# A transformer layer in one kernel: the square weights of the feed-forward are loaded and split in the fill, the routing works in other tiles, and every engine's list of steps is written anew

## The reference

```python
y  = moe(x, cond)        # 8 experts (64 wide) and a shared one (128 wide), top 2 of softmax((x@wt.T + cond@wg.T) / 2)
                         # each: (leaky(x @ gate) * (x @ up)) @ down, weighted by the route
q, k, v = split(y @ W_qkv + b_qkv)
a  = (q @ k.T / sqrt(128*32)) * band(32) @ v          # no softmax
x1 = x + layer_norm(a) * ln_w + ln_b
n  = layer_norm(x1) * g_norm
Q  = l2norm(n @ Wq) * q_scale                         # 16 heads of 64
K, V = l2norm([null_k; n @ Wk]) * k_scale, [null_v; n @ Wv]    # one key and value for all heads
bias = mlp(relative position)                         # 255 positions -> 16 heads
o  = softmax(8 * Q @ K.T + bias, causal and masked) @ V
z  = layer_norm(o @ Wout) * g_out
h  = silu(z @ w1.T * s1) * (z @ w2.T * s2)
h  = gelu(h @ h1.T * t1);  h = gelu(h @ h2.T * t2)    # h1, h2: 512 x 512, the square weights
out = x1 + h @ w3.T * s3
```

## Time and profile before

| | us |
|---|---|
| median of 3 runs | 715.47 |
| lowest, highest | 715.38, 719.20 |
| the profiled execution | 719.08 |
| its span, first to last instruction | 717.1 |
| mean granted clock of TensorE | 0.983 of full |

### The profile page before, as it was taken

How to read it: one execution, slowest core, us unless ns; L and a number is a source line. 1 busy time by engine, 2 the same in 40 slices (tenths; PEclk the granted TensorE clock), 3 DMA queues, 4 the chain that set the end, 5 groups by cost and what they waited for, 6 DMA issues and landing times.

```text
span 717.1 us, 20509 instructions
## 1 busy us (share of the span) xinstructions
PE 679.9 (95%) x7232; PEld 537.5 (75%) x7232; DVE 547.5 (76%) x1719; ACT 528.1 (74%) x1629; POOL 359.6 (50%) x410
## 2 busy tenths in 40 slices
PE   5986979999999999999999999999999999899997
PEld 5855757667876778768876778777876687778897
DVE  5476999898769878698759878698759977886441
ACT  3224679579876897579876898589875989899753
POOL 3013777572549343863549344863558456932100
PEclk9898988999999999999999999999999999999999
DMA  8042400300031000400031000400040000000000
GB/s 284 9 111 90 123 2 16 82 22 1 2 87 60 1 2 12 134 3 1 3 104 43 1 3 24 122 2 1 2 118 30 1 1 25 16 17 1 17 8 8
DMA packets 33587, 28.50 MB, mean 40 GB/s; under 512 B 4288, under 2 KB 29008, under 8 KB 33104
## 3 DMA queue, kind: packets, MB, share of 16 engines
q1 hardware_dynamic: 33184, 27.19, 13.2%
q10 hardware_dynamic: 304, 0.01, 0.0%
HBM read 23.90 MB, written 3.29 MB: 38 GB/s over the span
## 4 chain that ended last, share of the span: by engine, by line
PE 57%; DVE 14%; ACT 9%; issue 7%; POOL 4%; DVEq 0%; ACTq 0%; POOLq 0%
PE ps_M L1314 30%; PE ps_z L1466 8%; DVE sb_sm L1187 5%; PE ps_S L1453 5%; PE ps_S L1438 4%; PE ps_M L1367 4%; PE ps_M L1498 3%; ACT sb_sm L830 3%; PE ps_S L1422 2%; PE ps_M L1397 2%; ACT sb_hT L795 2%; POOL sb_rq L697 1%; DVE sb_nmx L1194 1%; DVE sb_hAl L1024 1%; POOL sb_biasm L707 1%
## 5 line engine op out<-in xcount | busy, mean ns | idle before, releaser
L830 ACT ACTIVATE sb_sm<-sb_sm,sb_nmx 128x65 f32<-128x65 f32 (+3 forms) x512 | 178.1, 352 | 14.4 <-DVE sb_nmx L1194 14.1
L715 POOL TENSOR_TENSOR sb_sm<-sb_sm,sb_rden 128x128 f32<-128x128 f32 (+3 forms) x128 | 93.2, 738 | 126.4 <-DVE sb_rden L1198 126.1
L707 POOL TENSOR_TENSOR sb_biasm<-sb_bias,sb_maskn 128x128 f32<-128x128 f32 (+3 forms) x128 | 113.0, 894 | 49.6 <-DVE sb_maskn L1159 26.5
L1187 DVE SCALAR_TENSOR_TENSOR sb_sm<-ps_S,sb_rq,sb_biasm 128x65 f32<-128x65 f32 (+3 forms) x512 | 112.2, 292 | 24.0 <-PE ps_S L1438 19.5
L697 POOL TENSOR_TENSOR sb_rq<-sb_qss,sb_mhalf 128x16 f32<-128x16 f32 x32 | 93.6, 2949 | 28.8 <-DVE sb_qss L1169 28.8
L830 ACT ACTIVATION_READ_ACCUMULATOR sb_sm<-sb_sm,sb_nmx 128x1 f32 x512 | 97.1, 190 | 0.0
L1466 PE MATMUL ps_z<-sb_wout,sb_oT 128*128 128x128 f32 x512 | 69.1, 282 | 0.0
L1466 PEld LDWEIGHTS ps_z<-sb_wout,sb_oT 128*128 128x128 f32 x512 | 64.4, 193 | 4.3 <-ACT sb_oT L842 0.8
L842 ACT ACTIVATE sb_oT<-ps_S,sb_cols 128x256 f32<-128x256 f32 x128 | 52.9, 467 | 16.5 <-PE ps_S L1453 13.1
L1194 DVE TENSOR_REDUCE sb_nmx<-sb_sm 128x4 f32<-128x132 f32 (+3 forms) x128 | 59.3, 475 | 0.3
L767 ACT ACTIVATE sb_gs<-ps_M 128x512 f32<-128x512 f32 x39 | 23.2, 596 | 46.2 <-PE ps_M L1314 46.1
(11 more groups left out here) (267 smaller groups left out, 1708.6 us busy)
## 6 DMA issues: line engine op xcount, KB each, us to landing
sb_hA<-routes SPq DMA_DIRECT2D x48, 128.0 KB, 3.6
sb_vrep<-values SPq DMA_DIRECT2D x16, 256.0 KB
sb_xg<-in_xT SPq DMA_DIRECT2D x8, 256.0 KB, 3.4
sb_xs<-in_x SPq DMA_DIRECT2D x8, 256.0 KB, 6.8
sb_qs<-in_xT SPq DMA_DIRECT2D x1, 2048.0 KB, 10.5
sb_hA<-in_h SPq DMA_DIRECT2D x2, 1024.0 KB, 7.2
out_y<-sb_res SPq DMA_DIRECT2D x7, 256.0 KB, 7.0
values<-sb_vs SPq DMA_DIRECT2D x16, 64.0 KB
```

The costliest lines, as they stand in the source:

```text
L707: pool.tensor_tensor(masked_bias(j % 4)[:, :, 1:wide], relative(bias0, i), maskn[:, j // 4, 0:wide - 1].unsqueeze(1).broadcast_to([128, 4, ...
L715: pool.tensor_tensor(p, p, stat(rden, g, j).unsqueeze(2).broadcast_to([128, 4, wide - 1]), ALU.mult)\
L830: ins = act.activation(p[:, t], p[:, t], ACT.Exp, bias=least[:, t:t + 1], accum_out=total[:, t:t + 1])
L1187: ins = dve.scalar_tensor_tensor(scored(g, j)[:, t], bank(g, "sim", n, odd)[:, first:first + wide], rq[:, col:col + 1], masked_bias(j % 4) ...
```

## The change

1. The routing's scratch moves out of hA into tiles that are not yet in use: pieces of x1 and of vrep (the spread values). For that `vb` (the spread of the values) of group 0 waits until the routing is done, and the x1 of group 2 is written only after the route weights have been turned.
2. So hA is free from the start: h1 and w12 are fetched right behind the mask in the prologue of SP, and h2 after SP has waited for h1's low part; only then follow the store and the 16 loads of the turned bias. The step `hw` is gone, and `PARTS` has h1 ahead of w12: `ph.3`/`pl.3` is now h1, `.4` w12, `.5` h2, and all six are in the fill.
3. The lists of all engines and all kinds of pass are written anew. The numbers of lines behind the table are larger by one to six.

```diff
 ORDER = {
     "pe fill": """
-        lg.0 warm.0-2 pb.0-1 warm.3-6 rw.0 lg.1-2 exp.0-1 lg.3-4 exp.2 pb.2 lg.5-7 pb.3 exp.3-4 down.0 qkv.0
...
+        lg.0 pb.0 warm.0-1 pb.1 warm.2 lg.1-2 rw.0 exp.0 lg.3 exp.1 lg.4 exp.2 lg.5 exp.3 lg.6-7 warm.3 pb.2
...
-        lgt, *rt = (hA[:, i // 2, i % 2 * 256:(i % 2 + 1) * 256] for i in range(8))
+        in_rows, in_spread = x1[:].rearrange("p r b d -> p (r b d)"), vrep[:].rearrange("p n i d -> p (n i d)")
+        lgt, *rt = (t[:, n * 256:(n + 1) * 256] for t, n in ((in_spread, 0), (in_spread, 1), (in_rows, 4), (in_rows, 2),
+                                                             (in_spread, 2), (in_rows, 3), (in_spread, 3), (in_rows, 5)))
...
-        PARTS = ("wqkv", "wkv2", "wq2", "w12", "h1", "h2")
+        PARTS = ("wqkv", "wkv2", "wq2", "h1", "w12", "h2")
...
             sp.dma_start(mask[:].rearrange("p b s -> p (b s)"), a["mask"][0:GT].unsqueeze(0).broadcast_to([128, GT]))\
                 .then_inc(mask_loaded.sem, 16)
+            fetch("h1", raw["h1"])
+            fetch("w12", raw["w12"])
+            sp.wait_ge(parts_low["h1"], 1)
+            fetch("h2", raw["h2"])
 
 
             sp.wait_ge(pa, 5)
...
             fetch("wout", wout[:])
-            fetch("w12", raw["w12"])
             fetch("w3", w3[:])
-
-            def load_square(g, k):
-                sp.wait_ge(*((routes_psum.sem, 1), (parts_low["h1"], 1))[k])
-                fetch(("h1", "h2")[k], raw["h1"])
...
             def spread_values(g, half):
                 sp.wait_ge(v_stored.sem, v_stored.at(g, 32))
+                if g == 0:
+                    sp.wait_ge(routed, 2 * ROUTE_OPS)
...
+                if g == 2:
+                    dve.wait_ge(routes_psum.sem, 1)
                 dve.tensor_tensor(x1[:, g % 3], mixture, xs[:], ALU.add).then_inc(own_x.sem, 1)
```

More of the change, by code:

```diff
@@ L60 @@
     "pe fill": """
-        lg.0 warm.0-2 pb.0-1 warm.3-6 rw.0 lg.1-2 exp.0-1 lg.3-4 exp.2 pb.2 lg.5-7 pb.3 exp.3-4 down.0 qkv.0
-        scores.0 mix.0 warm.7 fl.0-1 warm.8-10 fl.2 warm.11-13 xnT.0 warm.14 wr.0 warm.15-16 q.0 kv.0 q.1-4
-        qs.0-3 q.5-7 kT.0 warm.17 qs.4-7 warm.18-21
+        lg.0 pb.0 warm.0-1 pb.1 warm.2 lg.1-2 rw.0 exp.0 lg.3 exp.1 lg.4 exp.2 lg.5 exp.3 lg.6-7 warm.3 pb.2
+        exp.4 pb.3 down.0 qkv.0 scores.0 warm.4 mix.0 warm.5-8 fl.0 warm.9-15 fl.1 warm.16-17 fl.2 xnT.0
@@ L64 @@
+        warm.18-20 wr.0 q.0 kv.0 q.1-3 warm.21 q.4 qs.0-3 q.5-7 kT.0 qs.4-7
     """,
     "pe start": """
-        rw.0 exp.0 sim.0-1 exp.1-3 sim.2 exp.4 down.0 sim.3-4 qkv.0 scores.0 mix.0 PV.0 sim.5-6 z.0 xnT.0 PV.1
-        q.0 z.1 sim.7 z.2 kv.0 q.1 PV.2 z.3 q.2-3 z.4 PV.3 q.4 qs.0-3 q.5-7 z.5 qs.4-7 kT.0 z.6-7
+        sim.0 rw.0 exp.0-1 sim.1 exp.2-3 sim.2 exp.4 down.0 sim.3 qkv.0 scores.0 sim.4 mix.0 PV.0 z.0 sim.5-6
+        z.1 xnT.0 PV.1 q.0 sim.7 z.2 q.1 kv.0 z.3 PV.2 q.2-3 z.4 PV.3 q.4 qs.0-3 q.5-7 z.5 qs.4-7 kT.0 z.6-7
@@ L68 @@
     """,
     "pe steady": """
-        sim.0 exp.0-3 sim.1 exp.4 down.0 zT.0 sim.2-3 qkv.0 l1.0 sim.4 l1.1 sim.5 l1.2-3 scores.0 l2.0-3 mix.0
-        PV.0 l3.0-2 sim.6-7 xnT.0 l3.3 kv.0 z.0 q.0 z.1 PV.1 l4.0 PV.2 q.1-2 z.2 q.3-4 qs.0-3 q.5-7 z.3 qs.4-7
-        kT.0 z.4 PV.3 z.5-7
+        sim.0 exp.0-1 sim.1 exp.2-4 down.0 zT.0 sim.2-3 qkv.0 l1.0 sim.4 l1.1 sim.5 l1.2-3 scores.0 l2.0-3 mix.0
+        PV.0 l3.0-2 sim.6-7 xnT.0 l3.3 z.0 kv.0 q.0-1 z.1 PV.1 q.2 l4.0 z.2 PV.2 q.3-4 qs.0-3 q.5-7 z.3 qs.4-7
@@ L73 @@
+        z.4 kT.0 PV.3 z.5-7
     """,
     "pe seventh": """
-        sim.0-1 exp.0 sim.2 exp.1-4 down.0 sim.3 zT.0 sim.4 qkv.0 scores.0 l1.0 sim.5 l1.1-3 mix.0 PV.0 l2.0
-        sim.6 l2.1 z.0 l2.2 xnT.0 PV.1 z.1 q.0 sim.7 q.1-2 l2.3 q.3 kv.0 q.4 qs.0-3 q.5 z.2 q.6-7 z.3 qs.4-7
-        l3.0 PV.2 l3.1 PV.3 z.4-5 kT.0 z.6-7
+        sim.0-1 exp.0-1 sim.2-3 exp.2-4 down.0 zT.0 sim.4 qkv.0 scores.0 l1.0-1 sim.5 l1.2-3 mix.0 PV.0 l2.0-1
+        sim.6 l2.2 PV.1 xnT.0 z.0-1 q.0 sim.7 q.1 l2.3 q.2-4 qs.0-3 kv.0 q.5-7 z.2-3 qs.4-7 l3.0 PV.2 l3.1 PV.3
@@ L111 @@
     """,
     "dve fill": """
-        cg.0 pb.0 rt.0 x0.0 pb.1 rt.1-4 rw.0 pl.0 wl.0 pb.2 exp.0 pb.3 exp.1 nk.0 exp.2 rt.5 exp.3 pl.1 rt.6
-        exp.4 rt.7 down.0 xl.0 rt.8 maskn.0 qkv.0 scores.0 mix.0 pl.2 ln1.0 rt.9 xnT.0 pl.3 nk.1 q.0 kv.0 q.1-4
-        vs.0 q.5-7 ssq.0 ssc.0
+        cg.0 pb.0 rt.0 nk.0 pb.1 rt.1-3 x0.0 rt.4 rw.0 pb.2 wl.0 pl.0 exp.0 pb.3 maskn.0 exp.1 pl.1-2 exp.2-3
+        rt.5 pl.3 rt.6 exp.4 rt.7 down.0 rt.8 qkv.0 scores.0 pl.4 mix.0 ln1.0 nk.1 rt.9 pl.5 xnT.0 q.0 kv.0
@@ L116 @@
+        q.1-2 vs.0 q.3-7 ssq.0 ssc.0 xl.0
     """,
     "dve start": """
[L118 to L121 removed]
@@ L122 @@
-        q.1-3 pl.5 q.4 vs.0 q.5 ssq.0 ssc.0 q.6-7
+        rw.0 xl.0 exp.0 sim.0 exp.1 max.0 exp.2 max.1 inv.0 exp.3 sim.1 max.2-3 exp.4 inv.1 sim.2 inv.2 tp.0
+        inv.3 max.4 down.0 tp.1-2 inv.4 max.5 sim.3 qkv.0 scores.0 max.6-7 tp.3 mix.0 sim.4 inv.5 ln1.0 max.8
+        tp.4 inv.6 max.9 inv.7 tp.5 inv.8 tp.6 sim.5 inv.9 tp.7 max.10 sim.6 max.11 maskn.0 xnT.0 inv.10 max.12
+        tp.8-9 max.13 inv.11 tp.10 sim.7 inv.12 tp.11-12 max.14 inv.13 q.0 max.15 q.1 inv.14 tp.13-14 inv.15
+        tp.15 kv.0 q.2 vs.0 q.3-5 ssq.0 ssc.0 q.6-7
```

96 lines of the change are left out of this document (47 added, 49 removed).

## The result

The changed kernel is slower: 726.49 us median of 4 runs (724.65 to 728.27) against 715.57 (715.38 to 719.2), ratio 1.0132 with a 95% interval of 1.01 to 1.0164: 1.3%, small but clear of the noise. The forecast was 711.9 us with a range of 706 to 718. The profiled execution took 726.6 us (span 724.7, clock 0.993).

The account below looks back on a forecast made before the run. TensorE was taken to bound the middle passes; in the fill and first pass, dependent steps and the clock. Gains of 0.8 (transpose start), 2.0 (clock) and 0.8 (first pass), 3.6 us, took 715.47 to 711.9, range 706 to 718.

Parts of the forecast that it names:

- (g): Five middle passes: 0 change, bounds 2.8 us gained and a loss as in the last rival.
- the last rival: Middle passes slower: weights land late behind output store and spread, five passes lose about 1.6 us each; 719.9 us, chance 0.17.
- The sign that the rival named: Middle passes: the slower case would show as VectorE's expert product waiting for a DMA in every pass.
- (a): Fill: splits of h1, w12 and h2 moved there are hidden, h1's by `down` by about 0.3 us; cost 0.
- (b): Fill: logits products spread between experts may spare TensorE a 1.2 GHz stretch; 0.4 us gained, bounds 1.1 gained, 1.0 lost.
- (c): Fill, layer norm: GpSimd's slow first add leaves the chain because the add of x and bias precedes it; 0.9 us gained.
- (d): Fill: turned bias's store waits behind h2, its loads land at 52.0, xn's transpose starts at 58.9, no slack.
- the rival built on it: Fill: h2 takes 9.5 us, transpose up to 3.8 us late, eating the gain; 715 us, range 713 to 717, chance 0.27.
- (e): Fill: hole filled, so full clock; 1.15 us gained from transpose to q.0, 0.9 behind; together 2.0, bounds 0 and 3.2.
- (f): First pass: VectorE loses 4.6 us of work, but GpSimd's chain sets time; 0.8 us gained, bounds 0 and 4.6.
- The sum: Fill and first pass: 0.8 + 2.0 + 0.8 = 3.6 us gained, taken from the median 715.47 to give 711.9.

Follow-up runs that it names:

- e1: Changed kernel with SyncE's middle-pass row put back to the order of the kernel before (values, x, weights, then spread and output): 714.26 us, ratio 0.9961.
- e3: Kernel before with only the first spread of the values moved ahead of the x and weight loads in SyncE's middle pass: 720.78 us, ratio 1.0045.
- e6: e5 with the first-pass lists of the kernel before too, leaving out the moved splits and load steps: 712.94 us, ratio 0.9952.
- e7: Kernel before with the changed middle-pass lists of TensorE, ScalarE, VectorE and GpSimd, SyncE's row and all else as before: 713.07 us, ratio 0.9952.
- e8: Kernel before with GpSimd's add of x and the norm's bias moved ahead of the first layer norm in the fill: 715.82 us, ratio 0.9981.
- e12: e7 with eleven more TensorE warm-up steps in the hole before the second layer norm's transposes: 711.93 us, ratio 0.9951.
- e10: e6 with four more early warm-up steps in TensorE's fill before x has landed: 714.5 us, ratio 0.9973.
- e5: e1 with the lists of the kernel before for the seventh pass, the last and the drain, all five engines: 714.47 us, ratio 0.9947.
- e11: e6 with three of GpSimd's query-norm powers in the first pass replaced by products: 714.63 us, ratio 0.997.
- e4: Changed kernel with the lists of the kernel before for middle, seventh, last pass and drain, all engines; fill and first pass changed: 716.96 us, ratio 1.0009.

## Why the prediction was wrong, step by step

**The step that failed is (g),** the middle passes at 0, with the loss left to the last rival at 0.17. The place was right: the first spread of the values, ahead of x and the weights on SyncE. I followed the weights there, found 2.2 us of slack and made the whole rival hang on it. Of x, which stands between the spread and the weights in the same row, I never worked out when it is wanted. It is wanted 6.7 to 7.1 us after its issue in the changed kernel (10.3 before) and lands after 6.9 to 9.2. The rival also charged the row with the spread's 0.55 us and its 3.0 us of waiting, and nothing for the store of the output, although it names it. In the new lists that store holds the values and x back for 6.8 us in each pass. The sign that the rival named, VectorE's expert product waiting for a DMA, did show in four passes, with 0.4 to 0.65 us; the first and longest wait was the one for x. The rival's price was 8 us for five passes; the row cost 12.2 (e1).

**The lack of loss at one boundary** also belongs here: at 212.3 ScalarE waited only 0.24 us. The loss begins only when x lands after it is wanted, and 2 us more or less of a DMA's landing decide it.

**(a) Hidden splits: right.** `down` took 4.56 us in a piece with h1's subtraction before the last expert product, 4.45 in e3 without it; and the last expert product started at 37.47 (forecast 38.8). e6 against e7 (712.94 and 713.07) puts the whole new fill, the moved splits with it, at nothing.

**(b) The experts and their clock: 0.4 forecast to be gained, 1.5 lost against most traces of the old fill.** I took the slow stretch of 32 to 35 for a property of the old order. From the first expert product to `down` the old fill takes 13.0 us in three traces (e3, e8, e12), 14.5 in e7 and 16.0 only in the execution that I had. The changed fill takes 14.3 to 17.3 in all nine of its traces, and in each the first product has 0.78 us, in none of the old ones (0.48). The bound on the side of a loss, 1.0, was passed; that fewer warm-ups are the reason isn't shown, as e10 put them back and gained nothing.

**(c) The first add: right in size, wrong in reason.** From the split of y, the experts' result, to the transposes it is 17.95 us instead of 18.85; e8 shows that the step I named does not bring it.

**(d) The turned bias: the wait did not decide.** The store of the bias, 16 KB, did wait for h2's 1 MB ahead of it: it took 4.6 us and landed 0.2 after h2, where before it took 1.45 with nothing so large ahead. The loads went out from 41.4 to 48.9 (forecast 42.1 and 7.5 on), the products waited 1.82 us for them, and the transpose started at 57.6 (forecast 58.9), 0.61 us later than TensorE was free for it, released by ScalarE. h2 landed after 4.8 us, not 9.5, and the rival built on it falls.

**(e) The clock after the hole: right in its first part.** q.0 came 2.58 us after the transposes began (forecast 2.6), with the clock at 1.00 from 52 to 62. e12 shows it alone: 1.4 us in the trace. The second part, 0.9 for the products behind q.0, was there only against the profiled execution: from q.0 to VectorE's first score step it took 16.5 us, e3, e7 and e8 15.6 with the same fill, and the changed kernel 15.4.

**(f) The first pass: 0.8 forecast to be gained, 0.9 lost,** 0.6 of it by the new order (e5 against e6). That VectorE's 4.6 us are not time was right (e6). That GpSimd sets the pass was only half of it (e11).

**The sum** for the fill and the first pass, 3.6 us, met the measured 3.44 (135.97 to 132.53) by luck. I carried a saving over from an execution of 719.08 to a median of 715.47, though this execution owed its 3.6 us more to stretches at half clock: 3.1 us from the first expert to `down` beyond e3, e8 and e12, and 0.9 behind q.0. Against those traces, 1.5 lost in (b) and 0.9 in (f) stand against 0.9 gained in (c) and about 1 in (e). That is no gain, and e4 measured none.

**What adds up,** from medians: 12.2 us for SyncE's row (e1), 2.7 gained by the other engines' middle lists (715.75 to 713.07, e7), 0.9 for the fill and first pass (716.09 to 716.96, e4, within its uncertainty); 716.1 + 12.2 - 2.7 + 0.9 = 726.5, measured 726.49. The 12.2 is itself the distance from e1 to 726.49, so the sum tests only that e7's and e4's parts give e1's time: 714.3, measured 714.26. That agreement is closer than the medians' uncertainty, some 2 us. The seventh and last pass together are 0.9 in the traces and nothing in the medians.

## What to carry to other kernels

When an order changes on a queue that sends DMAs, work out for every transfer behind the moved one when it goes out, when it lands and when it is wanted, in the new lists, and begin with the ones closest behind it. Ask of the moved one itself when its data are ready: a transfer that waits at the head of a queue holds back all behind it, here for 6.8 us. When one profiled execution stands above the median, find what it owes this to before a saving is read from the same rows; a stretch of slow clock that other executions don't have is no saving. Put back one row at a time: a large rewrite can hold a gain of 2.7 us and a loss of 12.2.

## What the runs showed of the hardware

A 256 KB load of x in the middle passes landed 2.7 to 4.3 us after its issue with the spread of the values behind it. With this 256 KB spread right ahead of it on the same queue it landed after 6.9 to 9.2 us in the changed kernel and after 7.8 to 10.0 in e3, where one took 5.1. From these numbers the wait behind the spread is an estimated 4 to 7 us. The Trainium skill, in DMA: Bandwidth & Descriptors, "Queues, rings and completion order", has descriptors consumed in ring order on each engine. The traces agree: in the changed fill the 16 KB store of the bias, sent right behind h2's 1 MB, landed 0.2 us after it. Half clock after the 6.28 us hole came in all four traces with it (the clock was 0.79 from 50 to 66 in each); with the hole filled it came in one of ten (e1, 0.89). Executions of one kernel differ by 2 to 8 us. Two traces with the same old fill, of e3 and of the kernel before, start the second pass at 131.75 and 135.97, and the 4.2 us between them arise before the first pass's first score step (75.63 and 79.94), where the stretches at half clock fall on other products in each.
